# Scores and turned scores of a step issued alternately on eight 32-row tiles of TensorE

## The reference, cut to what matters

```python
WS, SHIFT, NH, FF, L = 7, 3, 3, 4, 49
win = _window_partition(jnp.roll(x, (-SHIFT, -SHIFT), axis=(1, 2)))   # windows of 49 positions
h = _layernorm(win, ln1_g, ln1_b)
q, k, v = ((h @ w).reshape(-1, L, NH, 8) for w in (wq, wk, wv))       # 3 heads of 8
attn = jnp.einsum('nqhd,nkhd->nhqk', q, k) / jnp.sqrt(8.0)
attn = softmax(attn + mask)
out = jnp.einsum('nhqk,nkhd->nqhd', attn, v) @ wo + bo
```

## Time and profile before

| | us |
|---|---|
| median of 3 runs | 3509.89 |
| lowest, highest | 3506.67, 3512.7 |
| span of the profiled execution | 3515.2 |
| TensorE matmuls busy in it | 3115.1 (89%) |
| VectorE busy | 1704.2 (48%) |
| ScalarE busy | 1625.4 (46%) |

### The profile page before, as it was taken

How to read it: one execution, slowest core, us unless ns; L and a number is a source line. 1 busy time by engine, 2 the same in 40 slices (tenths; PEclk the granted TensorE clock), 3 DMA queues, 4 the chain that set the end, 5 groups by cost and what they waited for, 6 DMA issues and landing times.

```text
span 3515.2 us, 110460 instructions
## 1 busy us (share of the span) xinstructions
PE 3115.1 (89%) x49194; PEld 1970.0 (56%) x49194; DVE 1704.2 (48%) x2740; ACT 1625.4 (46%) x2883; POOL 359.9 (10%) x574
## 2 busy tenths in 40 slices
PE   6968889888898888998989889998899988999888
PEld 3536646466465574554745647546465474564744
DVE  5424555355553545444454545635455354563544
ACT  3542354633546325554355443463544535445344
POOL 4510010000100001001000011000110001100011
PEclk9989999999999999999999999999999999999999
DMA  2322000110001100110001100011000210001100
GB/s 80 67 49 51 2 15 4 50 31 2 16 4 50 32 2 16 22 50 13 2 17 33 50 1 2 17 51 32 2 2 17 51 32 1 2 18 33 32 1 15
DMA packets 31252, 84.83 MB, mean 24 GB/s; under 512 B 24818, under 2 KB 25954, under 8 KB 26930
## 3 DMA queue, kind: packets, MB, share of 16 engines
q1 hardware_dynamic: 29506, 72.56, 8.7%
q0 software_dynamic: 1280, 5.21, 0.5%
HBM read 61.70 MB, written 14.84 MB: 22 GB/s over the span
## 4 chain that ended last, share of the span: by engine, by line
PE 72%; ACT 12%; DVE 5%; issue 5%; SPq 4%; DMA 3%; ACTq 0%; DVEq 0%
PE ps L1131 72%; ACT lv L719 2%; SPq L495 2%; ACT rs L724 2%; ACT area_ty L853 2%; DMA area_ty<-area_hz 1%; ACT sq L707 1%; SPq L510 1%; DMA area_hz<-f_all 1%; DVE xs L1102 1%; ACT area_ty L845 1%; ACT sq L705 1%; DVE area_ty L1098 1%; ACT area_ty L805 1%; ACT area_ty L811 1%
## 5 line engine op out<-in xcount | busy, mean ns | idle before, releaser
L1131 PE MATMUL ps<-area_hz 32*64 32x147 f32 (+2 forms) x7180 | 357.7, 285 | 84.7 <-DMA area_hz<-f_all 28.8
L1131 PE MATMUL ps<-area_ty,area_hz 113*64 113x49 f32 (+1 forms) x10240 | 393.5, 250 | 22.1 <-DMA area_ty<-area_hz 20.1
L829 ACT ACTIVATE area_hz<-ps 121x384 f32<-121x384 f32 (+2 forms) x256 | 129.6, 519 | 582.9 <-PE ps L1131 582.9
L1131 PE MATMUL ps<-sq,keep_sb 64*64 64x392 f32 (+1 forms) x1728 | 335.1, 531 | 71.0 <-ACT sq L707 44.0
L1131 PEld LDWEIGHTS ps<-area_hz 32*64 32x64 f32 (+2 forms) x7180 | 287.8, 154 | 191.2 <-issue 168.7
L1131 PEld LDWEIGHTS ps<-area_ty,area_hz 113*64 113x64 f32 (+1 forms) x10240 | 332.0, 135 | 104.1 <-issue 103.5
L1131 PE MATMUL ps<-area_ty,g_sb 56*112 56x192 f32 (+1 forms) x3712 | 311.8, 321 | 26.0 <-DVE area_ty L1074 19.7
L977 DVE TENSOR_REDUCE area_hz<-ps 113x12 f32<-113x588 f32 x256 | 196.4, 770 | 273.7 <-PE ps L1131 272.9
L944 DVE TENSOR_TENSOR area_ty<-ps,rs 128x392 f32<-128x392 f32 (+2 forms) x304 | 197.5, 650 | 260.0 <-ACT rs L724 259.9
L1131 PEld LDWEIGHTS ps<-area_ty,g_sb 56*112 56x112 f32 x3712 | 293.3, 173 | 44.7 <-issue 44.0
L1074 DVE COPY area_ty<-ps 120x896 f32<-120x896 f32 (+1 forms) x192 | 164.8, 858 | 262.8 <-PE ps L1131 262.8
(11 more groups left out here) (123 smaller groups left out, 4306.2 us busy)
## 6 DMA issues: line engine op xcount, KB each, us to landing
area_hz<-f_all SPq DMA_DIRECT2D x16, 2541.0 KB
xw<-x_in SPq DMA_DIRECT2D x8, 1568.0 KB, 6.5
y_out<-xs SPq DMA_DIRECT2D x32, 252.0 KB
f_all<-piece POOLq DMA_DIRECT2D x16, 317.6 KB, 3.4
area_ty<-area_hz SPq DMA_DIRECT2D x256, 4.6 KB
area_hz<-raw_in SPq DMA_DIRECT2D x1, 2894.0 KB, 9.4
g_sb<-g_in SPq DMA_DIRECT2D x6, 355.2 KB
g_sb<-g_in SPq DMA_DIRECT2D x2, 710.5 KB
```

The lines of the kernel that those rows point to most:

```text
L829: act.activation(dst, src, ACT.Relu if st in (ST_H, ST_F2) else ACT.Copy).then_inc(sc_kept, 1)
L1131: return pe.matmul(o, a, b, start=start, stop=stop)
```

## The change

Scores and turned scores of a step leave as one block: for each i first the four score matmuls, then the four turned ones. The turned ones take the other column half for each image (`far`), so the eight of one i lie on eight tiles of 32 rows and 64 columns. All waits of both stand ahead of the block. The stationary operands have 49 columns, except in the steps that first touch a bank (64 there). As the turned scores' partitions are swapped, so are those of `ring`: values, ones and the `wv` matmuls' destinations.

```diff
         def value_blocks(b, jj):
-            base = ring[64 * jj:64 * jj + L, b, :, 32 * jj:32 * jj + 1]
+            far = 1 - jj
+            base = ring[64 * far:64 * far + L, b, :, 32 * jj:32 * jj + 1]
...
-                def quadrants(bank, still, moving, w, dst):
+                def scores(bank, u, w, dst, n):
                     for j in range(QI):
                         g, jj = j // 2, j % 2
                         r = slice(RW * j, RW * j + RW)
-                        ins = mm(ps[PADL * jj:PADL * jj + PADL, bank + g, dst:dst + NH * L],
-                                 still[r, w, :], moving[r, w, :])
-                    return ins
+                        yield mm(ps[PADL * jj:PADL * jj + n, bank + g, dst:dst + NH * L],
+                                 qs[r, u % 2, w, 0:n], km[r, u % 2, w, :])
+
+                def turned_scores(t, w, dst, n):
+                    for j in range(QI):
+                        g, far = j // 2, 1 - j % 2
+                        r = slice(RW * j, RW * j + RW)
+                        yield mm(ps[PADL * far:PADL * far + n, 2 + g, dst:dst + NH * L],
+                                 ks[r, t % 3, w, 0:n], qm[r, t % 3, w, :])
...
-                        pe.sem_inc(passed_pe, 1)
-                        for i in range(2):
-                            ins = quadrants(score_bank(k), qs[:, u % 2], km[:, u % 2], 2 * (k % 4) + i, NH * L * i)
-                        ins.then_inc(scored, 1)
                     if 0 <= n < STEPS:
                         if dw == 0:
                             pe.wait_ge(max_rows, q * NW * 64 + 64 * t + 64)
                         if n >= 1:
                             pe.wait_ge(exped, q * STEPS + n)
                         else:
                             pe.wait_ge(maxed, q * STEPS + AHEAD)
+                    if 0 <= k < STEPS or 0 <= n < STEPS:
                         pe.sem_inc(passed_pe, 1)
                         for i in range(2):
-                            ins = quadrants(2, ks[:, t % 3], qm[:, t % 3], 2 * dw + i, NH * L * i)
-                        ins.then_inc(cross, 1)
+                            if 0 <= k < STEPS:
+                                for ins in scores(score_bank(k), u, 2 * (k % 4) + i, NH * L * i,
+                                                  PADL if k < AHEAD else L):
+                                    pass
+                                if i == 1:
+                                    ins.then_inc(scored, 1)
+                            if 0 <= n < STEPS:
+                                for ins in turned_scores(t, 2 * dw + i, NH * L * i, L if n else PADL):
+                                    pass
+                                if i == 1:
+                                    ins.then_inc(cross, 1)
```

More of the change, by code:

```diff
@@ L551, in ones_in_ring @@
                 for jj in range(2):
-                    r = slice(64 * jj, 64 * jj + L)
+                    r = slice(64 - 64 * jj, 64 - 64 * jj + L)
                     for h, c in ((0, 24), (1, 25), (2, 26), (0, 27)):
@@ L1008, in window_attention @@
                                 value_blocks(u % 2, jj),
-                                ps[64 * jj:64 * jj + L, 7, 0:NW * 2 * C].rearrange(
+                                ps[64 - 64 * jj:64 - 64 * jj + L, 7, 0:NW * 2 * C].rearrange(
                                     "p (u h d) -> p u h d", h=NH, d=DH))
@@ L1217, in window_attention @@
                     k = n + AHEAD
+                    u = k // 4
                     if 0 <= k < STEPS:
-                        u = k // 4
                         if k % 4 == 0:
@@ L1287, in window_attention @@
                             for jj in range(2):
-                                ins = mm(ps[PADL * jj:PADL * jj + L, 7, 2 * C * w:2 * C * w + 2 * C],
+                                far = PADL - PADL * jj
+                                ins = mm(ps[far:far + L, 7, 2 * C * w:2 * C * w + 2 * C],
                                          xh[:, TW * u + L * w:TW * u + L * w + L], wv[:, jj, :])
```

## The result

| | before | after |
|---|---|---|
| median, us | 3508.3 | 3463.0 |
| lowest, highest of four runs each | 3506.2, 3512.7 | 3461.3, 3466.9 |
| span of the profiled execution | 3515.2 | 3461.5 |

The kernel is faster by 45 us: the ratio is 0.9864, 95% interval 0.9843 to 0.9884. The prediction was 3474 (3450 to 3500).

A forecast was written before the change was run, and what follows sets the result against it. TensorE was taken to bound the kernel, busy 89% of the span and throughout the attention's window rows. Shorter blocks gave -50 us, clock falls +14, together -36: 3509.9 - 36 = 3474 us, range 3450 to 3500.

The forecast's parts named there:

- The block: Scores and turned scores on eight tiles take about 0.68 us up to the weighing, against 1.17: 0.49 us less per step.
- rival A: The block is not twice as fast but takes 1.09 us, and the kernel gets slower, 3534 us; chance 9%.
- Point 1: At dw = 0, t = 3 to 5, `wq` waits for VectorE's layer-norm product, so gain 0 there.
- Point 2: TensorE's wait for the DMAs of the maxima: 5.2 us on average from maxima copy to next scores, limiting the gain.
- Point 3: At n = 24 ScalarE's exponential can't come earlier; the block of n = 25 waits, so 0.98 us shrinks to 0.38.
- The sum: Gains over a quad's window rows in the attention, without the clock: -6.3 us per quad, -50 us in eight.
- The clock: Nine more falls to half clock behind TensorE's waits at n = 0, 4 and 8, 1.6 us each: +14 us.
- The total: Whole kernel: -36 us together, giving 3474 us against the median.
- The signs: Forecast wrong if the block exceeds 0.75 us, window rows reach 11.7, or clock falls spread into t = 3 to 6.
- C: Only part of the overlap: a block of 0.8 to 0.9 us, gain 5 to 20 us, about 3495 us; chance 13%.
- B: Every step keeps its whole saving: 208 x 0.49 = 102 us, 3408 us; chance 6%.

The follow-up runs named there:

- experiment 1: The changed kernel with turned scores in the same column half as the scores, so four tiles and not eight: 3533.9 us, ratio 1.0056.
- experiment 6: The changed kernel with VectorE's layer-norm product moved ahead of the addition into `xw` at dw = 0: 3465.9 us, ratio 0.9872.
- experiment 7: The changed kernel with two of the four DMAs of each window row's maxima issued by GpSimd from quad 1 on: 3447.8 us, ratio 0.9823.
- experiment 8: The kernel before the change, with two of the four maxima DMAs on GpSimd's queue from quad 1 on, nothing else: 3510.3 us, ratio 0.9983.
- experiment 9: The kernel before the change, with the layer-norm product ahead of the addition into `xw`, nothing else: 3520.6 us, ratio 1.0015.
- experiment 10: The changed kernel with maxima DMAs on two queues and the layer-norm product ahead of the addition into `xw`: 3440.4 us, ratio 0.9784.
- experiment 11: The changed kernel with maxima DMAs on two queues and the layer-norm product ahead of the addition only at t = 3 to 5: 3429.3 us, ratio 0.9775.
- experiment 12: The changed kernel with maxima DMAs on two queues, product first at all t, and 2 and 1 unread matmuls at n = 0 and 4: 3438.6 us.
- experiment 2: The changed kernel with all eight score matmuls of a step issued before the eight turned ones, not alternately: 3468.0 us, ratio 0.9868.
- experiment 3: The changed kernel with stationaries of 64 columns throughout, not 49: 3466.4 us, ratio 0.9866.
- experiment 4: The changed kernel with 6, 4 and 2 unread matmuls ahead of the DMA waits at n = 0, 4 and 8: 3498.7 us, ratio 0.9954.
- experiment 5: The changed kernel with 3, 2 and 1 unread matmuls ahead of the DMA waits at n = 0, 4 and 8: 3453.5 us, ratio 0.9838.

## Why the prediction was right, point by point

- **The block**: 0.68 us predicted, 0.67 measured, by the rate of the earlier trace rows. On four tiles it is 1.14 (experiment 1), near rival A's 1.09, and then the kernel is slower, 3534, the time that A gives. The Trainium skill's floor of about 25 ns from start to start (TensorE: Matmul & The Clock Gate, Part 1) would have made the block an estimated 1.0; here 32 records start within 0.47 us (583.76 to 584.22), 15 ns apart on average, so the measurement goes against it for this case. The Trainium skill also says that different row tiles cannot access one PSUM bank at the same time (TensorEngine Tiling (Array Packing), Gotcha 1). The row tiles of images 0 and 1 write one bank, in two column halves, and here and before all four score tiles start within 0.02 us; the measurement decides.
- **Point 1** (VectorE at dw = 0): 7.25 to the copy predicted, 7.23 measured (7.26 from the block's first score); experiment 6 took the wait away and found 6.70. Right.
- **Point 2** (the DMAs): 5.2 on average was predicted at t = 3 to 6, and the mean of the 32 is 5.2. Behind the window rows t = 1 and 2 I had 4.8 and 5.2, and 4.8 and 5.2 came out. Ahead of t = 1 I kept quad 1's prompt 4.44; the mean is 4.99. What point 2 left out is the reduce at n = 0, whose wait ends some 0.2 us before that for the DMAs; it cost nothing here and shows in experiments 7 to 12.
- **Point 3** (the exponential at n = 24): it does wait, 0.30 us; t = 6 is 10.54 and not 10.74.
- **The sum**: -50 without the clock, from quad 1. Quad by quad the level after was right, 80.9 predicted (88.79 less the fall of 1.6 in it, less 6.3) and 81.2 measured. But the other quads of the kernel before had later DMAs than quad 1, in quad 0 at t = 3 up to 7.21 from copy to turned scores, so that the mean there was 88.2 and not 87.2, and the gain is 56.
- **The clock**: +14 us for nine more falls, five of them at n = 0 and four at n = 4 and 8. The five at n = 0 came in every profile of the kernel. At n = 4 and 8 the number follows how late the DMAs come, and that differs from execution to execution: eight in the profile after, four in experiment 2, one in experiment 3. The idle time ahead of n = 4 was 1.16 to 2.15 us where a fall followed in the profile after and 0.94 and 0.95 where none did; in experiment 2 1.14 to 2.00 and 0.93 to 1.16; in experiment 3 1.70 and 0.77 to 1.48. So the falls cost 23.5, 15.7 and 9.6 us more than before, 16 on average. One costs 1.8 and not 1.6, in part because some last 6 us and not 3. Experiments 4 and 5, in which none is left, show that they come from TensorE's waits there.
- **The total**: predicted -36, measured -45. In the profile after, -56.2 + 23.5 - 4.7 gives -37.4 for the attention; that this is near -36 is luck, since work and falls are both off, in opposite ways. Over the three profiles of the kernel it is -56.2 + 16.2 - 4.7 = -44.7, the fall of the median, and nothing is left for the stages outside the attention, where I had predicted nothing. Experiments 2 and 3 had 12 and 20 us more than the change outside the attention, 6 and 16 less in it falls included, and nearly the same median. So the 9 us beyond the forecast are 6 of later DMAs in the kernel before, which I had read from one quad, and 5 of stalls, which I had not counted, less 2 of clock. The stalls appear in all three profiles without the block (three, and one and three in experiments 8 and 9) and not in the three of the changed kernel, though experiment 12, which has the block, shows one; why they went, no run shows.
- **The signs**: none of the three by which I would have been wrong came: the block is 0.67, the window rows of t = 3 to 5 take 12.45, and no fall stands at t = 3 to 6 in the profile after or in those of experiments 2 and 3.
- **Rivals**: A and C are out by the block's 0.67. B is out by the window rows of t = 3 to 5, 12.45 and not 13.66 - 4 x 0.49 = 11.70. With the waits for the product and the maxima taken away (experiment 11) they reach 11.66: these two waits held what B had counted.

## What to carry to other kernels

A tighter block on the busiest engine is worth what the next wait leaves: count per loop body which wait takes over, and then look at that wait in its own right. Here moving one VectorE operation and splitting four DMAs over two queues took the ratio from 0.9864 to 0.9775, two thirds of the block's gain on top of it. Ask each time which wait ends next: at n = 0 the wait for the reduce ended only 0.2 us before that for the DMAs, and two queues won no more than that. An instruction moved forward in a queue must be followed through the whole loop, also where the loop's other work has ended and its inputs come late: at the tail it blocked what stood behind it and gave back 10.4 of the 12.5 us that it had won. Idle time of TensorE that grows from 1.5 to 2.7 us is not only idle time: price the slow stretch that can follow it. And as such stretches differ in number from execution to execution, take more than one profile before you explain a few microseconds by them: three profiles of one kernel in effect had 16, 12 and 9.

## What was not expected of the hardware

- TensorE started turned scores ahead of twelve score records that stand before them in its program (573.59 against 573.70 to 573.96), as their tiles were free. On eight tiles the order in the program made no difference, 0.9868 against 0.9864.
- Six unread float32 matmuls of 128 x 448 took 4.75 us, 0.79 each; in experiment 5 three took 2.52.
- Two queues shortened the landing of four DMAs of 4.6 KB from 4.3 to 2.7 us after the copy: SyncE's issues are 0.77 us apart, and nearly the whole difference is two of them.
- The wait of 2.7 us at n = 0 had a fall behind it in all eight quads of all three profiles of the changed kernel. At n = 4, where TensorE is idle for 0.8 to 2.2 us as the DMAs come more or less late, six, four and one of eight had. Waits filled with unread matmuls had none, in 24 of 24 places in each of experiments 4 and 5.
